# Sparse cross-attention: one of four last sum measures moved from ScalarE to VectorE

## The reference

```python
qh, kh, vh = (_split_heads(a @ W + b) for ...)          # 16 heads of 16; q from _layernorm(x), k and v from ctx
scores = jnp.einsum('bhqd,bhkd->bhqk', qh, kh) * scale
def sparsemax(x):
    x = x - jnp.max(x, axis=-1, keepdims=True)
    zs = -jnp.sort(-x, axis=-1)
    rho = jnp.arange(1, L + 1, dtype=x.dtype)
    cssv = jnp.cumsum(zs, axis=-1) - 1.0
    support = zs > cssv / rho
    k = jnp.maximum(jnp.sum(support, axis=-1, keepdims=True), 1)
    tau = jnp.take_along_axis(cssv, k - 1, axis=-1) / k.astype(x.dtype)
    return jnp.clip(x - tau, 0.0)
out = jnp.einsum('bhqk,bhkd->bhqd', sparsemax(scores), vh)
x = x + jnp.tanh(g_xattn[0]) * (out @ Wo + bo)
x = x + jnp.tanh(g_ffn[0]) * moe(_layernorm(x))          # 8 experts, top 2
```

## Time and profile before

| | us |
|---|---|
| median of 3 runs | 7428.7 |
| lowest and highest of them | 7425.35, 7432.42 |
| the profiled execution, its own time | 7425.2 |
| its span in the trace | 7423.3 |
| TensorE, VectorE, ScalarE, GpSimd busy | 5646.4, 5977.4, 5842.5, 2210.4 |

### The profile page before, as it was taken

One profiled execution on the slowest core, in us unless ns is written; L12 is line 12 of the kernel. 1 busy time (PEld: TensorE's weight loads), 2 busy tenths in 40 slices (PEclk: granted clock), 3 DMA queues, 4 the chain that ended last, 5 costly groups with the idle time before them and its releaser, 6 DMA issues. The chain is left out here.

```text
span 7423.3 us, 165050 instructions
## 1 busy us (share of the span) xinstructions
PE 5646.4 (76%) x20864; PEld 1924.1 (26%) x20864; DVE 5977.4 (81%) x49467; ACT 5842.5 (79%) x13220; POOL 2210.4 (30%) x10037
## 2 busy tenths in 40 slices
PE   8976777776777777767777777677777775999999
PEld 5541111111111111111111111111111111666666
DVE  5559989999998999999999999899999995444443
ACT  2328999999999999999999999899999996222222
POOL 2223333333333333333333333333333332000000
PEclk9986666666666666666666666666666666999999
DMA  6651111111111111111111111111111112111110
GB/s 203 225 194 30 30 30 31 32 30 30 33 31 31 30 31 30 30 29 30 30 32 30 32 30 33 27 31 32 31 32 31 33 33 62 49 37 48 51 37 23
DMA packets 315591, 344.02 MB, mean 46 GB/s; under 512 B 113912, under 2 KB 238464, under 8 KB 314240
## 3 DMA queue, kind: packets, MB, share of 16 engines
q1 hardware_dynamic: 311936, 324.40, 15.9%
q0 software_dynamic: 2304, 8.39, 0.3%
HBM read 212.38 MB, written 120.10 MB: 45 GB/s over the span
## 5 line engine op out<-in xcount | busy, mean ns | idle before, releaser
L856 DVE MAX8 a_cand<-a_scores 128x8 f32<-128x42 f32 (+1 forms) x38912 | 4359.1, 193 | 296.2 <-issue 222.9
L619 ACT ACTIVATE a_junk_act<-a_cand,a_ntau 128x304 f32<-128x304 f32 (+1 forms) x4096 | 2066.8, 522 | 112.3 <-POOL a_ntau L931 50.5
L589 PE MATMUL a_ring<-a_q,a_k 99*128 99x512 bf16 (+1 forms) x3328 | 1478.7, 560 | 800.7 <-ACT a_scores L654 594.2
L534 PE MATMUL a_out<-a_attn,a_v 128*16 128x512 f32 (+1 forms) x6656 | 1404.2, 767 | 575.2 <-ACT a_attn L658 575.2
L654 ACT COPY a_scores<-a_ring 128x1024 f32<-128x1024 f32 (+1 forms) x2048 | 1612.2, 830 | 176.8 <-PE a_ring L585 110.1
L658 ACT ACTIVATE a_attn<-a_ring 128x1024 f32<-128x1024 f32 (+1 forms) x1792 | 1653.4, 974 | 2.5 <-PE a_ring L589 2.0
L585 PE MATMUL a_ring<-a_k,a_q 96*128 96x512 bf16 (+1 forms) x4096 | 1393.6, 471 | 71.6 <-DVE a_ident L679 32.9
L619 ACT ACTIVATION_READ_ACCUMULATOR a_junk_act<-a_cand,a_ntau 128x1 f32 x4096 | 845.6, 206 | 0.0
L585 PEld LDWEIGHTS a_ring<-a_k,a_q 96*128 96x128 bf16 x4096 | 391.9, 118 | 1472.7 <-issue 696.5
L589 PEld LDWEIGHTS a_ring<-a_q,a_k 99*128 99x128 bf16 (+1 forms) x3328 | 290.1, 119 | 1669.7 <-ACT a_scores L654 978.9
L1192 ACT ACTIVATE e_hid<-e_hid_ps,e_b_in 128x512 f32<-128x512 f32 x256 | 173.1, 687 | 667.7 <-PE e_hid_ps L1139 667.4
(11 more groups left out here) (171 smaller groups left out, 5777.0 us busy)
## 6 DMA issues: line engine op xcount, KB each, us to landing
a_k<-k_parts SPq DMA_DIRECT2D x1536, 50.0 KB
k_parts<-p_ks SPq DMA_DIRECT2D x48, 800.5 KB, 7.5
o_parts<-a_o SPq DMA_DIRECT2D x1024, 32.0 KB, 1.6
e_o<-o_parts SPq DMA_DIRECT2D x64, 512.0 KB, 6.6
p_ctx<-in_ctx_t SPq DMA_DIRECT2D x16, 1601.0 KB, 8.5
v_heads<-p_v SPq DMA_DIRECT2D x16, 1536.0 KB
a_q<-q_parts SPq DMA_DIRECT2D x1536, 16.0 KB
a_v<-v_heads SPq DMA_DIRECT2D x256, 96.0 KB
```

What stands on the lines that cost most here:

```text
L534: mm = nc.tensor.matmul(out_ps[at:at + HEAD_DIM], v_st[0:rows, u, c], attn[0:rows, k, (c % 2) * BANK:(c % 2 + 1) * BANK], start=c < 4, sto ...
L589: mm = nc.tensor.matmul(at[0:rows, m * BANK:(m + 1) * BANK], k_st[0:SCORE_ROWS + TAU_ROWS, ut, c * P:c * P + rows], q_st[0:SCORE_ROWS + TA ...
L619: ins = nc.scalar.activation(into[:, t].rearrange("p (a b) -> p a b", b=CHUNKS), cand[:, u % SLOTS, t, 0:w], ACT.Relu, bias=ntau[:, u % 2, ...
L856: ins = V.max(cand[:, u % SLOTS, t, :, c], scores[:, u % SLOTS, t, lo:hi])
```

## The change

Round 3 of an item is shared. ScalarE measures tiles 0 to 2 (`ACT_LAST` = 3). VectorE measures tile 3, one SCALAR_TENSOR_TENSOR with accumulator over the 304 candidates, in quarter 0 of step i for item i-2: `beside(0)` yields three times, so that eight MAX8 are ahead, waits for `tau_tried` (all three moves of that item), measures, yields, and only then goes on to `start`. GpSimd's `last_step` waits for the new semaphore `last_summed` ahead of `excess_made`.

```diff
--- before.py
+++ after.py
@@ -60,6 +60,7 @@
 EXACT = 3e-5
 BEFORE_LAST = 3e-4
 GENERAL_STEPS = 26
+ACT_LAST = 3
 
 
 def project_program(nc, x, ctx_t, wq, bq, wk, bk, wv, bv, ident_in, q_parts, k_parts, v_heads):
@@ -468,6 +469,7 @@
         counted = sem("counted")
         tau_tried = sem("tau_tried")
         excess_made = sem("excess_made")
+        last_summed = sem("last_summed")
         fall_made = sem("fall_made")
         inv_made = sem("inv_made")
         bad_ready = sem("bad_ready")
@@ -614,7 +616,7 @@
                     act.wait_ge(guessed, i + 1)
                 else:
                     act.wait_ge(tau_tried, (ROUNDS - 1) * i + r)
-                for t in range(TILES):
+                for t in range(ACT_LAST if r == ROUNDS - 1 else TILES):
                     w, into = (SECOND, junk_act0) if r == 0 else (8, junk_act)
                     ins = nc.scalar.activation(into[:, t].rearrange("p (a b) -> p a b", b=CHUNKS), cand[:, u % SLOTS, t, 0:w], ACT.Relu,
                                                bias=ntau[:, u % 2, t:t + 1], accum_out=excess[:, u % 2, r, t:t + 1])
@@ -833,6 +835,16 @@
                 def beside(t):
 
                     last, prev = (u - 2) % U, (u - 1) % U
+                    if t == 0 and has(i, 2):
+
+                        for _ in range(3):
+                            yield
+                        dve.wait_ge(tau_tried, (ROUNDS - 1) * (i - 1))
+                        for n in range(ACT_LAST, TILES):
+                            values, nt = cand[:, last % SLOTS, n], ntau[:, last % 2]
+                            V.scalar_tensor_tensor(out=view(junk, values, CAND, n), in0=values, scalar=nt[:, n:n + 1], in1=zeros_like(values), op0=ALU.add, op1=ALU.max,
+                                                   accum_out=excess[:, last % 2, ROUNDS - 1, n:n + 1]).then_inc(last_summed, 1)
+                        yield
                     if t == 0 and has(i, 1):
 
                         dve.wait_ge(cand_made, i)
@@ -886,6 +898,8 @@
                 def last_step(i, u):
 
                     nt = ntau[:, u % 2]
+                    pool.wait_ge(last_summed, (TILES - ACT_LAST) * (i + 1))
+                    pool.sem_inc(passed_pool, 1)
                     pool.wait_ge(excess_made, ROUNDS * i + ROUNDS)
                     pool.sem_inc(passed_pool, 1)
                     link(G.tensor_scalar(over[:], excess[:, u % 2, ROUNDS - 1], -1.0, None, ALU.add))
```

## The result

| | before | changed |
|---|---|---|
| median, us | 7429.0 (4 runs, 7425.4 to 7432.4) | 7368.8 (4 runs, 7368.2 to 7372.1) |
| profiled execution, us | 7425.2 | 7368.7 |
| span in the trace, us | 7423.3 | 7367.0 |

The ratio of the changed kernel's time to that of before is 0.992, with a 95% interval of 0.9903 to 0.9937. It is 0.8% faster, 60 us.

The account below looks back on a forecast made before the run. ScalarE and VectorE were taken to pace the attention pass in turns. Removing 156 us of VectorE's waits, adding 118 us of work and keeping 18 us gave -20 us from 7425.2, forecast 7406 us, range 7382 to 7445.

Parts of the forecast that it names:

- The bound: Attention pass: ScalarE-paced items (21.05 us) and VectorE-paced ones (20.26 us) take turns; VectorE waits 156 us in all.
- ScalarE's 0.535 us: ScalarE in each item: one measure less saves 0.535 us, so a ScalarE-paced item falls from 21.05 to 20.52 us.
- VectorE's price: VectorE in each item: the added measure costs 0.46 us, 118 us over 256 items (102 to 141).
- What is moved: L717 and `start` come 1.35 us later, behind eight MAX8 and the measure; the guess's delay stays hidden in ScalarE's slack.
- The waits that stay: VectorE still waits where TensorE is late before ScalarE has a lead: 0.07 us an item, 18 us.
- The sum: Whole kernel: -156 us of waits, +118 of new work, +18 of waits that stay, -20 us in all.
- The new waits: VectorE's wait for L949 before the measure and GpSimd's wait for the measure both cost 0.
- The guess's delay: ScalarE would wait 0.2 to 0.4 us for L728's guess in half of the items, hidden in its slack.
- Rival 3: All VectorE's waits go: 7371 us with a measure of 0.40 us, 7387 with 0.46; chance 0.12.
- Rival 1: ScalarE keeps no lead, waits of 0.2 to 0.3 us an item stay: slower, 7438 to 7464 us; chance 0.17.
- Rival 2: Item by item, no carry-over of waits: no measurable change, 7410 to 7438 us; chance 0.26.
- Rival 4: Different rounding changes which rows fall back; one pass more or less is under 10 us; no chance of its own.

Follow-up runs that it names:

- h: The changed kernel with VectorE's loop written over twelve items, not six: 7304.2 us against 7423.4 for the kernel before, ratio 0.9840.
- i_before_turn12: The kernel before with VectorE's loop written over twelve items, not six: 7425.8 us against 7427.9, ratio 1.0000.
- The experiment with one pair: The kernel before with all of the first guess (`start`) two MAX8 later and nothing else: 7419.0 us against 7423.6, ratio 0.9993.
- e_measure_at_once: The changed kernel without the three yields, the measure behind two MAX8: 7359.5 us against 7423.4 for the kernel before, ratio 0.9917.
- f_two_tiles: The changed kernel with two tiles measured on VectorE and two on ScalarE: 7519.6 us against 7423.6 for the kernel before, ratio 1.0128.
- l_all_turn18: The changed kernel with all four compute engines' loops over eighteen items: 7301.6 us against 7427.9 for the kernel before, ratio 0.9832.

## Why the prediction was right in kind and wrong in size

*The bound.* That two kinds of items take turns and that the gain lies in VectorE's waits was right: 156 us were estimated, the stages give 0.64 us an item, 164 us. The pair of h and i shows it by experiment: the same edit on VectorE gains 60 us in the changed kernel and nothing in the kernel before, where 56 us of freed time turn into waits. That the waits were 8 us more than the rows gave is the smallest of three errors of size. The loop turns 40 times in the trace and not 42, which changes nothing.

*ScalarE's 0.535 us.* As predicted: three measures and the next copy run from 2940.07 to 2941.66, 1.59 us, 0.53 each.

*VectorE's price, the first term that was mis-sized.* The record was forecast at 0.53 us and is 0.52, start to start 0.44 us (2940.82 to 2941.26). But quarter 0 grew by 0.39 us only, 100 us and not 118. Of the 18 us, 5 are the 0.46 that was taken for 0.44, and 13 are time ahead of L717 that is gone in its new place. The step that failed is "What is moved": it counted the eight MAX8 and the measure, and didn't ask whether L717 had waited for anything in its old place. The experiment with one pair shows it: 0.08 us an item less, with nothing changed but the place.

*The waits that stay, the second term.* 0.07 us an item was kept, 18 us. Measured are 3.7 us in the two wait rows, 0.03 us an item in the stages. The step that failed is in "The sum": it had VectorE wait whenever TensorE is late "before ScalarE has won a lead". The lead is there in every plain item. The paragraph on the guess had worked it out as 0.5 + 0.46 = 0.96 us; in the 138 items of the changed kernel in which TensorE isn't late, L742 starts a median 0.75 us behind its input, 0.72 us later than it could. In 43 items one late piece of 0.6 to 0.9 us stands ahead of the third measure; it uses the lead up, and in 31 of them L742 waits, but only for what goes beyond the lead, 0.15 us on the average. In no other item does it wait for more than 0.05 us; where TensorE is later still (36 items), a fallback makes VectorE later too.

*The sum* is then -164 + 100 + 8 = -56 us, with the stages' own numbers. Against the forecast of -20, the 36 us between are 18 us for the price of the measure, 10 us for the waits that stay, and 8 us for those that were there before. All three err the same way.

*The new waits.* VectorE's for L949 cost one piece of 2.0 us in the whole run, forecast 0. GpSimd's L905 waits for VectorE's measure in 68 items and for ScalarE in 186, and VectorE waits for nothing behind it, as forecast. ScalarE does: for L932 (the old L918) 18.9 us in 72 items, where it was 4.9 us in 6. The sign that its wait for L949 would be larger didn't come true, 33.8 us against 39.3. The lock that VectorE and GpSimd may share (the Trainium skill, "SBUF — State Buffer", section "SBUF: two separate sides") met nobody at the measure: in the item shown the two GpSimd records around it end at 2939.85 and start at 2941.96, and no GpSimd record overlaps any of the 256 measures.

*The guess's delay.* It was forecast that ScalarE would wait 0.2 to 0.4 us in half of the items. It waited 64.8 us in 70 items: 0.76 us each without the 12.2 us of the pass's first. Nothing of it that could be measured reached VectorE: e_measure_at_once, without most of the delay, is as fast. It does take lead from ScalarE, 0.75 us for 1.16.

*Rival 3* ("all waits go", 0.12) was what happened, and 7371 us, its lower bound, is 2 us from the measured time: not because the measure costs 0.40 us, but because it does so net. That it hits the time so closely is partly luck: it had the waits at 156 us and let all of them go, where 164 were there and 8 stayed. *Rival 1* (no lead kept) fell: its turning point was 0.15 us of waits that stay. *Rival 2* (item by item) fell too: waits carry over. *Rival 4* had no effect: 45 fallback passes before and after.

## What to carry to other kernels

When two engines take turns as the pace, work is worth moving as long as the one that receives it still waits, and the price is read from the waits that go, not from busy shares: here 100 us of new work on the fuller engine (81% busy) took 156 us of its waits away and brought 56 us. Halving or doubling the amount moved tells where the balance is; with two tiles moved there were no waits left to lose, and the price was paid in full. And before a chain is moved, ask whether its first instruction waits in its old place, and compare the slack at the meeting point with one late signal, not with the mean lateness.

## What the runs showed of the hardware

The skip of the fallback loop that is not entered (L802's branch to the next step) takes 0.53 us from branch to target in 214 of the 218 items of the kernel before that skip it and in 216 of 218 of the changed one (medians), and 0.20 us in 213 of 218 once VectorE's loop holds twelve steps, with the same instructions around it. On the timeline the idle time at the first MAX8 behind it is 0.72 us in the changed kernel

```profile
2952.09 0.74 DVE L868 MAX8 a_cand<-a_scores 128x8 f32<-128x42 f32 x6
2953.56 2.60 DVE L868 MAX8 a_cand<-a_scores 128x8 f32<-128x42 f32 x24 [0.72 <-issue]
```

and 0.39 us with twelve steps:

```profile
2928.75 0.74 DVE L868 MAX8 a_cand<-a_scores 128x8 f32<-128x42 f32 x6
2929.88 2.29 DVE L868 MAX8 a_cand<-a_scores 128x8 f32<-128x42 f32 x21 [0.39 <-issue]
```

In f_two_tiles it is 0.20 us at two of the six places in the body and 0.53 at the others, and in l_all_turn18 0.20 at eight of the eighteen. So it goes with where the code lies, not with the data; one measure more in each step of the body (f_two_tiles, also a wait of 3.0 us at each turn for 2.0) is enough to change it. A short branch doesn't always save the time: in i_before_turn12 it takes 0.20 us in 212 of 218 items, but at four of the twelve places the stretch from the cast to quarter 3, without a fallback, still takes 4.34 to 4.37 us, where it was 4.32 before; at seven it takes 4.0 to 4.1. The Trainium skill, "Runtime: NRT & Kernel Launch", section "Instruction fetch mechanics", says that an engine holds two pages of 256 instructions, filled in sequence, and that a branch to a target outside of them must fetch it first. The turn of the loop, 2.0 us of idle in the changed kernel, agrees with it: its body holds 912 MAX8 alone. What makes a skip inside the body cost 0.53 us in one layout and 0.20 in another, no run here settles.
